# A two-layer gated cross-attention and expert kernel: another order of TensorE's work in a step, and the row transfers of a pair of batches spread over two steps

## What is computed

```python
x = x + tanh(g_xattn[0]) * L0_xattn(_layernorm(x), ctx_512, Wq, Wkv, Wo)     # 16 heads of 8
x = x + tanh(g_ffn[0])   * L0_ffn(_layernorm(x), gate_w, w1, w2)             # top 2 of 8 experts, gelu
x = x + tanh(g_xattn[1]) * L1_xattn(_layernorm(x), ctx_512, ctx_512, Wq, bq, Wk, bk, Wv, bv, Wo, bo)
x = x + tanh(g_ffn[1])   * L1_ffn(_layernorm(x), Wr, br, W1, b1, W2, b2, gamma, beta)   # top 2 of 8, relu, layer norm
```

## Time and profile before

| | us |
|---|---|
| median of 3 runs | 573.4 (572.22 to 574.28) |
| the profiled execution | 571.19 |
| its span, first to last instruction | 569.4 |
| PE busy in it | 440.4 (77%) |
| DVE busy in it | 336.9 (59%) |
| POOL busy in it | 237.4 (42%) |
| ACT busy in it | 214.2 (38%) |
| mean granted clock of PE | 0.826 |

### The profile page before, as it was taken

The page is one execution under the profiler, slowest core; times in us unless marked ns, Lnnn a source line. Parts: engine busy times, 40 slices in busy tenths (PEclk is TensorE's granted clock), DMA queues, the critical chain, the costliest instruction groups (busy, mean ns, idle before and its releaser), DMA issues.

```text
span 569.4 us, 16851 instructions
## 1 busy us (share of the span) xinstructions
PE 440.4 (77%) x5346; PEld 334.9 (59%) x5350; DVE 336.9 (59%) x1255; ACT 214.2 (38%) x608; POOL 237.4 (42%) x378
## 2 busy tenths in 40 slices
PE   7788889878576899999478787877865799999300
PEld 4465455545444699998145555544544699999300
DVE  4678556755438656666338855754544756666493
ACT  4434323232232444442044432323221566666221
POOL 7023543453443144445102354435345244554456
PEclk9599785978855999999869968677875999999855
DMA  7791000000000122221200010000010122222241
GB/s 222 213 314 22 21 20 2 22 21 20 20 18 25 47 67 67 70 65 52 74 10 21 20 39 30 4 18 21 20 50 28 42 57 68 63 68 65 70 121 55
DMA packets 38672, 32.06 MB, mean 56 GB/s; under 512 B 6984, under 2 KB 32245, under 8 KB 38613
## 3 DMA queue, kind: packets, MB, share of 16 engines
q1 hardware_dynamic: 34069, 21.86, 14.0%
q0 software_dynamic: 4544, 9.41, 5.1%
HBM read 20.26 MB, written 10.99 MB: 55 GB/s over the span
## 4 chain that ended last, share of the span: by engine, by line
PE 53%; DVE 20%; issue 8%; another core or an unknown queue 8%; ACT 3%; POOL 3%; DMA 2%; DVEq 1%; POOLq 1%; ACTq 0%; SPq 0%
PE bank L671 49%; PE bank L674 4%; DVE room L1288 4%; DVE mx L1265 4%; ACT room L1052 2%; DVE room L1295 1%; DMA o_rows<-room,ids 1%; DVE v_s L1167 1%; POOL wa L648 1%; DVE x L1250 1%; DVE x L1302 1%; DVE wa L1497 1%; DVE fstats L1307 1%; DVE wa L1490 1%
## 5 line engine op out<-in xcount | busy, mean ns | idle before, releaser
L623 POOL DMA_INDIRECT o_rows<-room,ids x78 | 77.7, 996 | 101.0 <-DVE room L1438 37.2
L671 PE MATMUL bank<-room 128*128 128x128 f32 x624 | 83.8, 277 | 2.9 <-issue 2.0
L671 PE MATMUL bank<-wa,room 128*128 x624 | 83.0, 276 | 1.3 <-ACT room L1110 1.1
L671 PEld LDWEIGHTS bank<-room 128*128 128x128 f32 x624 | 75.7, 192 | 6.1 <-ACT room L1115 3.1
L671 PEld LDWEIGHTS bank<-wa,room 128*128 128x128 f32 x624 | 76.1, 192 | 2.0 <-issue 1.9
L576 POOL DMA_INDIRECT xg_rows<-xfa,slots x64 | 63.9, 998 | 32.0 <-issue 19.0
L1265 DVE TENSOR_REDUCE mx<-bank 128x4 f32<-128x324 f32 x128 | 54.4, 487 | 36.2 <-PE bank L671 36.2
L988 ACT ACTIVATE room<-bank 128x128 f32<-128x128 f32 (+1 forms) x110 | 31.2, 284 | 107.2 <-PE bank L674 104.7
L1288 DVE RECIPROCAL room<-bank 128x128 f32<-128x128 f32 x32 | 30.6, 956 | 60.6 <-remote 47.4
L1052 ACT ACTIVATE room<-bank 128x384 f32<-128x384 f32 x128 | 52.4, 495 | 27.0 <-PE bank L671 27.0
L1415 DVE COPY room<-wa 128x512 f32 x78 | 33.3, 427 | 39.2 <-issue 20.3
(11 more groups left out here) (191 smaller groups left out, 733.9 us busy)
## 6 DMA issues: line engine op xcount, KB each, us to landing
room<-xg_rows SPq DMA_DIRECT2D x78, 65.5 KB
wa<-in_L_ffn_w SPq DMA_DIRECT2D x1, 2048.0 KB, 10.1
wb<-in_L_ffn_W SPq DMA_DIRECT2D x1, 2048.0 KB, 17.1
ob<-o_rows SPq DMA_DIRECT2D x32, 64.0 KB, 1.9
wb<-o_rows SPq DMA_DIRECT2D x6, 256.0 KB, 4.5
o_rows<-room,ids POOLq DMA_INDIRECT x78
x<-in_x SPq DMA_DIRECT2D x4, 256.0 KB, 4.4
xg_rows<-xfa,slots POOLq DMA_INDIRECT x64
```

Source lines behind the costliest of these rows:

```text
L623: pool.indirect_dma_start(out=o_dram[l], in_=o_sb[t.slot(UN)][:, :], in_offset=None, out_offset=bass.IndirectOffsetOnAxis(ap=ids[t.slot(UN ...
L671: return pe.matmul(out_, lhsT, rhs, start=start, stop=stop)
```

## The change

It touches the attention stage alone, on three engines.

- PE: `turn_max` comes before `scores`, `less_max` and the turning of xn follow at once, and the output of b3 comes after them. The logits of b5 move from before the scores to behind the output, and `more_values` behind the logits. The ranks are made for pair s - 7 (`placed`) and not s - 6.
- DVE: the choice is made for pair s - 6 (`chosen`), at the end of odd steps, and the placing for pair s - 7, at the end of even steps. Logits and ranks are read earlier, right after `ons`. The kept values of layer 0 are those made in the step before. The second statistics of both batches of a pair are taken together.
- POOL: the count is that of `placed`. The four row transfers of a pair b (up to pair 11) go as two in step b + 8 (odd) and two in step b + 9 (even), behind POOL's other work in the step. The last two pairs go with four each, in steps 20 and 21, so that step 20 has six.

The numbers of instructions of each kind stay as they are. Cut to its core (the bodies of `choose`, `read_ranks` and `place` are those of the lines removed):

```diff
--- before.py
+++ after.py
         def live_pair(b):
             return b.c % 2 == 1 and live(b)
 
+        def due(s, n, last):
+
+            if s.c == B - 1 + last:
+                return Step(B - 1)
+            return Step(s.c - n) if live_pair(s.back(n)) and s.c - n < B - 1 else None
+
+        def chosen(s):
+            return due(s, 6, 5)
+
+        def placed(s):
+            return due(s, 7, 6)
+
 
 
 
...
 
                 def step(s):
-                    b4, b6, b7 = (s.back(n) for n in (4, 6, 7))
+                    b4, b8, b9 = (s.back(n) for n in (4, 8, 9))
                     if live_pair(b4):
                         S["f1"].wait(pool, b4)
                         rsqrt(S["rs2"], b4, frs[:, :, 1], frs[:, :, 0], fmv[:, :, 1], mhalf[:, 0:2])
@@ -599,18 +611,24 @@
                         pool.tensor_tensor(q_, two[:, :, 0], r_, ALU.mult).then_inc(rs.sem, 1)
                         rs.wait(pool, of, 3)
                         pool.tensor_scalar(nq, q_, -1.0, None, ALU.mult).then_inc(rs.sem, 1)
-                    if live_pair(b6):
-                        cu = S["cu"]
-                        S["rk"].wait(pool, b6)
+                    if placed(s):
+                        b, cu = placed(s), S["cu"]
+                        S["rk"].wait(pool, b)
                         pool.tensor_tensor(cum[:, :], cum[:, :], mb[:, 0, :], ALU.add).then_inc(cu.sem, 1)
-                        cu.wait(pool, b6, 1)
+                        cu.wait(pool, b, 1)
                         pool.tensor_tensor(cum[:, :], cum[:, :], mb[:, 1, :], ALU.add).then_inc(cu.sem, 1)
-                    ready = b6 if b6.c == B - 1 else b7
-                    if live_pair(ready) and (ready.c == B - 1) == (ready is b6):
-                        S["f4"].wait(pool, ready)
-                        S["f2"].wait(pool, ready)
-                        scatter(ready, 0)
-                        scatter(ready, 1)
+                    for b, js in ((b8, (0,)), (b9, (1,))):
+                        if live_pair(b) and b.c < B - 3:
+                            S["f4"].wait(pool, b)
+                            S["f2"].wait(pool, b)
+                            for j in js:
+                                scatter(b, j)
+                    if s.c >= B + 4:
+                        b = placed(s)
+                        S["f4"].wait(pool, b)
+                        S["f2"].wait(pool, b)
+                        scatter(b, 0)
+                        scatter(b, 1)
...
                         pe.wait_ge(v_kept, late_batch(s.c))
+                        if chosen(s):
+                            S["f3"].wait(pe, chosen(s), 1)
+                        if placed(s):
+                            S["f4"].wait(pe, placed(s), 1)
                         vals(0, late_batch(s.c), bank[7][:, 288:])
...
                     S["c2"].wait(pe, b)
+                    S["f3"].wait(pe, b.back(2), 1)
                     for j in range(2):
...
+                def ranks(b, s):
+
+                    S["f3"].wait(pe, b, 8)
+                    S["cu"].wait(pe, b.back(2))
+                    if live_pair(s.back(5)):
+                        S["c2"].wait(pe, s.back(5))
+                    if l == 0 and b.c == 1:
+                        hear(pe, "consts")
+                    r0, r1 = bank[7][:, 272:280], bank[7][:, 280:288]
+                    mm(r0, tri[:, :], mb[:, 0, :], True, False)
...
+                    mm(r1, onesb[:, :], cum[:, :], False, True).then_inc(S["rk"].sem, 1)
...
+                    if placed(s):
+                        ranks(placed(s), s)
+                    if live_pair(b5) and b5.c == B - 1:
                         logits(b5)
-                    if live_pair(b6):
-
-                        S["f3"].wait(pe, b6, 8)
-                        S["cu"].wait(pe, b6.back(2))
-                        if l == 0 and b6.c == 1:
-                            hear(pe, "consts")
-                        r0, r1 = bank[7][:, 272:280], bank[7][:, 280:288]
...
-                    if l == 0:
-                        more_values(s)
                     if live(b2):
+                        turn_max(b2)
                         scores(b2)
-                        turn_max(b2)
+                        less_max(b2)
+                    if live(s):
+                        S["xn"].wait(pe, s)
+                        tr(bank[4][:, NC * T:NC * T + P], xn[s.slot(2)][:, :], P).then_inc(S["t1"].sem, 1)
                     if live(b3):
                         S["rc"].wait(pe, b3)
                         o = bank[6][:, 2 * T:3 * T]
                         if l == 1:
                             mm(o, onesb[0:65, :], bo_3[:, :], True, False)
                         mm(o, ons[:, :], wo[l][:, :], l == 0, True).then_inc(S["wo"].sem, 1)
-                    if live(b2):
-                        less_max(b2)
-                    if live(s):
-                        S["xn"].wait(pe, s)
-                        tr(bank[4][:, NC * T:NC * T + P], xn[s.slot(2)][:, :], P).then_inc(S["t1"].sem, 1)
+                    if live_pair(b5) and b5.c < B - 1:
+                        if placed(s):
+                            S["f4"].wait(pe, placed(s), 1)
+                        if l == 0:
+                            pe.wait_ge(v_kept, min(s.c + 1, B))
+                        logits(b5)
+                    if l == 0:
+                        more_values(s)
                     if live_pair(b4):
                         S["f2"].wait(pe, b4)
                         if l == 0:
-                            pe.wait_ge(v_kept, min(s.c + 2, B))
-                        S["f4"].wait(pe, b4.back(2), 1)
+                            pe.wait_ge(v_kept, min(s.c + 1, B))
+                        if chosen(s):
+                            S["f3"].wait(pe, chosen(s), 1)
...
+                def read_logits(b):
+
+                    f3, raw = S["f3"], bank[7][:, 256:256 + 2 * E].rearrange("p (j e) -> p j e", j=2)
+                    S["lg"].wait(dve, b)
+                    if l == 0:
...
+                def choose(b):
...
+                    S["f4"].wait(dve, b.back(2))
+                    ohv = oh[:, :, :].rearrange("p (j k) e -> p j k e", k=2)
...
+                def read_ranks(b):
+
+                    S["rk"].wait(dve, b)
...
+                def place(b):
...
-                    if l == 0 and late_batch(s.c) is not None:
-                        dve.wait_ge(v_made, late_batch(s.c) + 1)
-                        values_kept(late_batch(s.c), bank[7][:, 288:])
-                    if live(b3):
                         rc.wait(dve, b3, 1)
                         S["wo"].wait(dve, b3.back(1))
                         dve.tensor_tensor(ons[:, :], bank[6][:, 0:T], den[:, :], ALU.mult).then_inc(rc.sem, 1)
+                    if placed(s):
+                        if chosen(s):
+                            S["lg"].wait(dve, chosen(s))
+                        read_ranks(placed(s))
+                    if chosen(s):
+                        read_logits(chosen(s))
+                    if l == 0 and late_batch(s.c - 1) is not None:
+                        dve.wait_ge(v_made, late_batch(s.c - 1) + 1)
+                        if live_pair(s.back(5)):
+                            S["c2"].wait(dve, s.back(5))
+                        values_kept(late_batch(s.c - 1), bank[7][:, 288:])
                     if live(Step(s.c + 2)):
                         stats_of(Step(s.c + 2))
                     if live(b3):
@@ -1301,58 +1393,19 @@
                         S["wo"].wait(dve, b3)
...
-                        f1, last = S["f1"], Step(b3.c | 1)
+                    if live_pair(b3):
+                        f1 = S["f1"]
                         S["x2"].wait(dve, b3)
-                        S["f2"].wait(dve, last.back(2))
-                        dve.bn_stats(fstats[:, b3.slot(2), :], x[:, seq(b3)]).then_inc(f1.sem, 1)
-                        if b3.c == last.c:
-                            for j in range(2):
-                                f1.wait(dve, last, j + 1)
-                                dve.bn_aggr(fmv[:, j, :], fstats[:, j, :]).then_inc(f1.sem, 1)
-                    if live_pair(b5):
-
...
+                        S["f2"].wait(dve, b3.back(2))
+                            dve.bn_stats(fstats[:, j, :], x[:, seq(b3.back(1 - j))]).then_inc(f1.sem, 1)
...
-                    if live_pair(b6):
...
+                            f1.wait(dve, b3, j + 1)
+                            dve.bn_aggr(fmv[:, j, :], fstats[:, j, :]).then_inc(f1.sem, 1)
+                    if placed(s):
+                        place(placed(s))
+                    if chosen(s):
+                        choose(chosen(s))
                 return step
```

More of the change, by code:

```diff
@@ new lines, in choose @@
+                def choose(b):
+                    f3, two = S["f3"], xfa[:, b.c - 1:b.c + 1, D + 1:D + 3]
+                    if l == 0 and b.c == 1:
+                        hear(dve, "consts")
+                    f3.wait(dve, b, 1)
```

(18 more changed lines are left out.)

64 lines of the change are left out of this document (19 added, 45 removed).

## The result

The changed kernel took 521.47 us (median, 516.21 to 521.99) where the kernel before took 573.19 beside it: a ratio of 0.908, 95% interval 0.902 to 0.914. Its profiled execution took 521.99 us, span 519.9, against 571.19 and 569.4.

A forecast was written before the change was run, and what follows sets the result against it. Attention steps were taken as bound by DVE, or by PE's small matmuls held beside transfer trains. The terms gave -11.1 us in each layer, 571.2 to 549.0 profiled, plus 2.2 for the median: 551, range 526 to 575.

The forecast's parts named there:

- Steps 2 to 8: Attention steps now without transfers: five at 5.6 to 5.95 us, two at 6.4; -7.4 us in each layer.
- Steps 9 to 16: Attention steps with a train of two transfers each: 8.8 us a step, -3.1 us in layer 0, -6.1 in layer 1.
- The first term: In steps 9 to 16, DVE's need where nothing is held: 6.4 us a step.
- The second and third together: In steps 9 to 16, 1.75 us a step for held small matmuls plus 0.65 for half clock.
- The crawl of seven groups: Scores and less_max on PE, six groups and one, at 0.6 to 0.75 us a group beside a train.
- Steps 17 and 18: Up to x of the last batch: about 12.0 us instead of 14.1 and 14.5; -2.1 and -2.5 us.
- Tail: Behind x of the last batch, POOL's longer queue delays the last count: +1.5 us in layer 0, +4.9 in layer 1.
- the hold: PE's small matmuls and signals delayed beside a transfer train until 0.95 us behind its end; 3.3 us for two transfers.
- Rival 1: Two transfers hold nothing that matters; steps 9 to 16 take DVE's 6.4 us each; median 513; chance 0.18.
- Rival 2: Steps 9 to 16: delay per pair stays 4.05 us however split, 9.15 us a step; median 557; chance 0.12.
- Rival 3: Steps 9 to 16: every train, two or four, holds 4 us in the worst place; median 589; chance 0.20.

The follow-up runs named there:

- the run with no transfers: Changed kernel with the transfers of pairs 1 to 11 sent behind the last step; steps 9 to 16 took 45.7 and 48.2 us; total time no measure.
- the old order with the split alone: Kernel before with each pair's four transfers sent as two in each of two steps, nothing else changed: 549.66 us, ratio 0.955; in a later set 516.9, 1.006.
- the first runs: The original measurement and profiles of the change: kernel before 573.19 us, changed kernel 521.47, ratio 0.908.
- the first set of experiments: Follow-ups with only the order changed (544.75 us), only the transfers split (549.66), or early pairs' transfers behind the last step; kernel before 576.15 us.
- the probe: Separate kernel without nearly all the computation: small matmuls beside trains of 0 to 8 indirect transfers; sixteen matmul passes took 0.44 us with any number.
- one-and-one: Changed kernel with a step's two transfers apart, one right behind scores_for_max, one where both were: 495.21 us, later 495.86 (ratio 0.966) and 495.81.

## Why the prediction was wrong in size and right in sign

**Steps 2 to 8**: -7.4 in each layer by the prediction, -10.5 and -9.3 measured. Steps 4 to 6 took 5.4 to 5.8 us, near the 5.5 to 5.95 foreseen; wrong were steps 7 and 8, which I let take 6.4 for DVE's work (5.8 and 5.7 in layer 0, 6.2 and 5.9 in layer 1).

**Steps 9 to 16**: -3.1 and -6.1 by the prediction, -19.6 and -17.1 measured. This is the step that failed. It made a step of 6.4 + 1.75 + 0.65 = 8.8 us; measured are 6.74 and 7.43. The first term is 5.71 and 6.02 (the run with no transfers). In layer 0 I had taken 5.55 us of DVE's work, from the kernel before, and 0.85 between its operations; it has 5.25 and 0.47. The second and third together, put at 2.4, are 1.03 and 1.40. Two things made them too large. The train doesn't start at 2.5 or 2.6 us after the maxima's start: the second norm's chain is 2.8 us long, as foreseen, but begins with the maxima, not ahead of them, so the train starts at 2.90 (321.67 - 318.77); in even steps it starts at 3.08. By then PE is in the midst of its scores, and they go out dense. The crawl of seven groups that my 1.75 rested on doesn't take place: in layer 0 single pauses remain, such as 0.46 us inside more_values, 2.7 us after the train's start at 91.27.

The premise under it, that a train holds back the small matmuls from its start, was misread from the rows themselves. Beside the train of the earlier trace rows, which starts at 348.73, and that of the earlier trace rows, which starts at 174.88, the kernel before has:

```profile
349.50 0.86 PE L671 MATMUL bank<-room,keep 128*32 128x128 f32 x24
...
174.72 1.04 PE L671 MATMUL bank<-wv,ctxT 65*32 65x32 f32 x43
```

Both run dense in the train's first 1.7 us. The pauses come later: the first group behind one starts 1.32 us after the train's start in the earlier trace rows, and 2.6 in the earlier trace rows, when a train of two, 2.36 long, would be over. What stays is late signals, 2.07 and 2.84 us from the train's start; x starts at 5.74 and 5.88 us after the maxima, where I had 6.9. And the clock, for which I took a third of the time at half, was at half for 6% and 18% of it (0.97 and 0.91), presumably because no crawl leaves PE behind; no run separates the two.

**Steps 17 and 18**: -2.1 and -2.5 by the prediction, -2.4 and -2.4 measured.

**Tail** (x of the last batch to the experts' first load): +1.5 and +4.9 by the prediction, +4.3 and +5.1 measured. The queue of POOL was read rightly for layer 1, with the count at 14.7 us behind x of the last batch, before 9.3, and the experts' load 9.1 behind that. For layer 0 I had said that the count waits for PE anyway. Without the hold its tail grew by 3.9 all the same (20.4 to 24.3), so there too the queue counts. Putting the count ahead of the last transfers took 1.3 and 1.1 us off the tails, and the profiled execution from a span of 490.9 to 486.6, of which 2.2 are an earlier start of step 2 that the edit doesn't explain. With a median of 489.4 us it is the best version measured, 3.4 below the changed kernel beside it; the intervals of the two ratios overlap.

**The range.** It was to go half-way to rivals 1 and 3, but half-way from 551 to 513 is 532 and to 589 is 570, not 526 and 575. The measured 521.5 lies outside either.

**The rivals.** Rival 1 named the right side, and its sign, scores that run dense beside two transfers, came in, but its mechanism was wrong where the forecast was scored: two transfers did cost the steps 8.2 and 11.2 us a layer; that the time came out between it and the forecast is due to terms of both. Where there is no hold its mechanism is true, and the gain is 19.6 us, because the kernel before has none to lose either. Rival 2, a hold per pair that stays, fell: 4 x 4.05 = 16.2 us by it, 8.2 and 11.2 measured, though the old order with the split alone (+16.9 in layer 0) came near it. Rival 3 fell: the position was not the worst but nearly the best. That 22.6 us of span (513.5 to 490.9) are gained without the hold, near the 22.2 forecast, is chance; the parts differ.

**What stays open**: what the hold is. It is in the first runs and the first set of experiments, and in none of the four later sets, with the same kernels and the same transfers. The record gives a chip's number for each set, 3 for the first set (576 us) and 3 for the second (514), then 7, 2 and 1; if the number names the same chip, the chip alone doesn't decide. The runs don't show whether it belongs to a place or an hour, or to the recording, in which those sets differ, nor whether it falls on trains alone or on each transfer, nor whether matmuls and transfers suffice for it, for the probe and one-and-one never met it. So the size of its cost is shown (no transfers against two or four in a step, in one set), its cause isn't.

## What to carry to other kernels

A loss read from a trace can belong to the conditions of the run and not to the kernel: before costing a change on it, have the kernel before profiled again at another time, and state the gain for both. Place the transfers of an engine that works in order so that what others wait for on it comes first, and cost a queue by what stands behind it: here, in the new order, two in each step beat four in every second one both with the hold and without; in the old order only with it. For the floor of a bound engine, take the transfers out of its steps and measure, instead of adding gaps to its busy time.

## What the runs showed of the hardware

Beside trains of indirect transfers on POOL, PE's signals came late, and with four in a train its small matmuls paused, in the runs up to the first set of experiments (groups of four 0.75 us apart, an exponential and x 2.07 and 2.84 us behind the train's start) and not in the four sets after it (six groups in 0.95 us beside the same train). The kernel before moved with this between 576 and 512 us, 11%, more than the change does (9% with the hold, 4% without).

The granted clock differed too. Without the hold, the kernel before had 0.84 in layer 1's steps 9 to 16 and took 59.1 us, the changed one 1.00 and 47.1; in layer 0 both had 1.00 and took 51.2 and 45.8. So of layer 1's 12.0 us some 6.6 are beyond what the change gave in layer 0, and the clock is the difference that the rows show. How much of that is the order's own isn't shown: each is one profiled execution, and one and one, the same kernel in two later sets, had 1.00 there once and 0.93 once (48.2 and 50.4 us).
